# A causal mask added on VectorE instead of by a product on TensorE, in a two-layer kernel on one NeuronCore

## The reference

```
h = rms(x, ln_w)
q = (h @ wq).reshape(B, S, 32, 64); k, v = ...(B, S, 8, 64)
q, k = rope(q, k)
scores = einsum('bqhd,bkhd->bhqk', q, repeat(k, 4)) / sqrt(64)
scores = where(tril(ones(S, S)), scores, -1e30)
attn = softmax(scores, -1)
o = einsum('bhqk,bkhd->bqhd', attn, v)
x = x + o @ wo
```

## Time and profile before

| | us |
|---|---|
| median of 3 runs | 2144.54 (2142.8 to 2145.47) |
| the profiled execution | 2131.14 |
| its span, first to last instruction | 2129.3 |
| the 64-wide attention, from its first scores to its last | 828 to 1752 |

### The profile page before, as it was taken

How to read it: one execution, slowest core, us unless ns; L and a number is a source line. 1 busy time by engine, 2 the same in 40 slices (tenths; PEclk the granted TensorE clock), 3 DMA queues, 4 the chain that set the end, 5 groups by cost and what they waited for, 6 DMA issues and landing times.

```text
span 2129.3 us, 37256 instructions
## 1 busy us (share of the span) xinstructions
PE 1830.0 (86%) x11178; PEld 1224.3 (57%) x11178; DVE 1241.0 (58%) x3257; ACT 1089.9 (51%) x2758; POOL 901.9 (42%) x1013
## 2 busy tenths in 40 slices
PE   4989899867777746999999999999999994799994
PEld 2656678633333324666766666766666673555552
DVE  5684554457576755666666666666666666622222
ACT  3324343336555414666666666666666661244442
POOL 3991000112221003444554444555444552588884
PEclk9999999859999978999999999999999995899997
DMA  5000020000001010000000000000000006355557
GB/s 150 1 1 1 1 60 1 0 1 1 1 1 40 1 42 1 1 1 0 0 0 0 0 0 0 0 0 0 0 0 0 0 0 235 104 83 84 82 83 165
DMA packets 61350, 60.76 MB, mean 29 GB/s; under 512 B 13136, under 2 KB 58320, under 8 KB 61264
## 3 DMA queue, kind: packets, MB, share of 16 engines
q0 software_dynamic: 15360, 20.98, 6.2%
q1 hardware_dynamic: 45904, 38.65, 5.6%
HBM read 40.48 MB, written 19.14 MB: 28 GB/s over the span
## 4 chain that ended last, share of the span: by engine, by line
PE 53%; DVE 17%; issue 12%; ACT 11%; POOL 4%; DMA 2%; DVEq 1%; ACTq 0%; SPq 0%; POOLq 0%
PE banks L1815 5%; PE banks L1796 5%; PE banks L1805 5%; PE banks L1773 4%; PE banks L1993 3%; PE banks L1869 3%; DVE con L1024 3%; PE banks L1618 3%; ACT wide_x L1437 2%; PE banks L1844 2%; POOL wdT L724 2%; PE banks L1827 2%; ACT wugT L1451 2%; PE banks L1784 2%; PE banks L1680 2%
## 5 line engine op out<-in xcount | busy, mean ns | idle before, releaser
L1773 PE MATMUL banks<-wide_k,wide_q 128*128 128x512 f32 (+3 forms) x1024 | 314.4, 389 | 0.5 <-ACT wide_k L1390 0.5
L1024 DVE TENSOR_REDUCE con<-banks 128x1 f32<-128x256 f32 (+3 forms) x512 | 246.3, 482 | 93.4 <-PE banks L1775 90.1
L656 POOL TENSOR_TENSOR wugT<-wugT,con 128x512 f32<-128x512 f32 (+1 forms) x256 | 236.5, 934 | 141.2 <-DVE con L1014 141.1
L1815 PE MATMUL banks<-late,xnT 128*128 (+1 forms) x512 | 195.9, 506 | 17.4 <-DVE xn L1038 14.2
L1773 PEld LDWEIGHTS banks<-wide_k,wide_q 128*128 128x128 f32 x1024 | 169.9, 191 | 55.3 <-issue 24.2
L1403 ACT ACTIVATE wugT<-banks,con 128x512 f32<-128x512 f32 (+1 forms) x256 | 161.7, 632 | 67.5 <-DVE con L1024 66.3
L1054 DVE TENSOR_REDUCE con<-banks 128x2 f32<-128x1024 f32 x128 | 154.7, 1214 | 65.1 <-PE banks L1857 64.2
L667 POOL TENSOR_TENSOR attn<-attn 128x320 f32<-128x320 f32 x128 | 111.7, 872 | 169.2 <-DVE attn L1002 165.8
L1796 PE MATMUL banks<-attn 128*64 128x256 f32 x1280 | 166.4, 389 | 0.0
L1044 DVE TENSOR_TENSOR wide_x<-attn,wide_x 128x256 fp32r<-128x256 f32 (+1 forms) x256 | 97.5, 421 | 110.1 <-ACT wide_x L1437 110.1
L1993 PE MATMUL banks<-w,late 128*128 x320 | 158.1, 617 | 2.5 <-issue 1.5
(11 more groups left out here) (309 smaller groups left out, 4168.6 us busy)
## 6 DMA issues: line engine op xcount, KB each, us to landing
w<-in_L_ffn_w_dram SPq DMA_DIRECT2D x32, 256.0 KB, 6.4
late<-in_L_ffn_w_dram SPq DMA_DIRECT2D x16, 256.0 KB, 6.3
y_rows<-wqkv1T SPq DMA_DIRECT2D x1, 2176.0 KB, 7.9
x<-in_L_attn_x_dram SPq DMA_DIRECT2D x4, 512.0 KB, 8.9
late<-in_L_ffn_wq_dram SPq DMA_DIRECT2D x2, 1024.0 KB, 7.2
late<-in_L_ffn_wo_dram SPq DMA_DIRECT2D x1, 2048.0 KB, 8.2
h_rows<-wugT SPq DMA_DIRECT2D x1, 2048.0 KB, 7.0
y_rows<-x SPq DMA_DIRECT2D x1, 2048.0 KB, 12.7
```

The lines of the kernel that those rows point to most:

```text
L656: nc.gpsimd.tensor_tensor(p, p, rinv[:, m:m + 1].to_broadcast([P, n]), ALU.mult).then_inc(at.sem["norm"], 1)
L1024: nc.vector.tensor_reduce(negmax[:, a:a + 1], bank[at.sbank(a)][:, 0:P * at.keys(at.row_of(a))], AX, ALU.max, negate=True).then_inc(at.sem ...
L1773: nc.tensor.matmul(sbank[:, 0:keys], wide_q[:, side, i, qcols], wide_k[:, side, w, 0:keys], start=(w == 0), stop=False)
L1815: ins = nc.tensor.matmul(bank[YBANK][:, 0:QKV], xnT[:, c, P * wide_tile(a):P * wide_tile(a) + P], w_qkv(n, c), start=(c == 0), stop=(c == ...
```

## The change

The mask product of TensorE goes. The second score product of a unit raises s_ps instead. A bf16 tile of 512 columns, `wide_mask`, takes the place of `causal`: zero in its first 384 columns, the causal tile in its last 128. In place of the maximum, DVE runs `tensor_tensor_reduce`: it adds the last columns of `wide_mask` (as many as the unit has keys) to the scores, multiplies by -1, writes the negated masked scores back over the scores in PSUM, and accumulates their minimum, with 3e38 as the starting value, into the unit's column of `negmax`, which is the negated maximum as before. Ahead of it stands a memset of an otherwise unused column of `negmax`. The exponential takes scale -1.0, as its input is negated now.

```diff
-        causal = sb("causal", [P, P], BF16)
+        wide_mask = sb("wide_mask", [P, S], BF16)
...
-            vch.inc(nc.vector.tensor_copy(causal[:], const("causal")))
+            nc.vector.memset(wide_mask[:, 0:S - P], 0.0)
+            vch.inc(nc.vector.tensor_copy(wide_mask[:, S - P:S], const("causal")))
...
                         v.wait_ge(at.sem["s_ps"], n * at.units + a + 1)
-                        nc.vector.tensor_reduce(negmax[:, a:a + 1],
-                                                bank[at.sbank(a)][:, 0:P * at.keys(at.row_of(a))],
-                                                AX, ALU.max, negate=True).then_inc(at.sem["max"], 1)
+                        nc.vector.memset(negmax[:, 16 + a:17 + a], 0.0)
+                        kk = P * at.keys(at.row_of(a))
+                        sc = bank[at.sbank(a)][:, 0:kk]
+                        nc.vector.tensor_tensor_reduce(sc, sc, wide_mask[:, S - kk:S], -1.0, 3.0e38, ALU.add, ALU.min,
+                                                       negmax[:, a:a + 1]).then_inc(at.sem["max"], 1)
...
                     nc.scalar.activation(at.prob(m)[:, 0:n], bank[at.sbank(m)][:, 0:n], ACT.Exp, bias=negmax[:, m:m + 1],
-                                         accum_out=rowsum[:, m:m + 1]).then_inc(at.sem["exp"], 1)
+                                         scale=-1.0, accum_out=rowsum[:, m:m + 1]).then_inc(at.sem["exp"], 1)
...
                         for w in range(2):
-                            nc.tensor.matmul(sbank[:, 0:keys], wide_q[:, side, i, qcols], wide_k[:, side, w, 0:keys],
-                                             start=(w == 0), stop=False)
-                        ins = nc.tensor.matmul(sbank[:, keys - P:keys], ident_h[:], causal[:], start=False, stop=True)
+                            ins = nc.tensor.matmul(sbank[:, 0:keys], wide_q[:, side, i, qcols], wide_k[:, side, w, 0:keys],
+                                                   start=(w == 0), stop=(w == 1))
                         ins.then_inc(at.sem["s_ps"], 1)
```

## The result

The changed kernel takes 2183.8 us (median of 4 runs, 2176.71 to 2185.14) against 2143.75: ratio 1.0195, 95% interval 1.0172 to 1.0218. It is slower by 40 us. The forecast was 2152, slower by 8, with a range up to 2178.

A forecast was written before the change was run, and what follows sets the result against it. A path of DVE and ACT was taken to bound 40% of the round, so +0.48 us there less 0.26 kept on TensorE gave +0.22 us a round, +7.2 us in all: 2152 us, range 2118 to 2178.

The forecast's parts named there:

- Together DVE gets 16 x 0.14 = 2.2 us more a round: On DVE: memset and accumulator's read at 0.07 us each, 16 times a round, bringing DVE to 21.9 of 29.2 us.
- B: Rival: DVE's small instructions cost as much as ACT's record shows, 0.4 us a maximum; +46 us, 2190 us; chance 0.09.
- TensorE's slot: On TensorE: each removed mask product frees 0.09 us, bounds 0.05 and 0.14; 16 a round, 512 in all.
- Where the gain is kept: On TensorE: only units 3, 4 and 15 keep their slot, 0.26 us a round; the other units win nothing.
- ACT and DVE path: Last wait chain of a round: 11.7 of 29.2 us on ACT and DVE alone, where PE work decides nothing.
- The main part of the new instruction: On DVE: add and running minimum written to PSUM take the maximum's time, 0 more; bounds -0.02 and +0.54 us for 512.
- The read and the memset: On DVE: 0.07 us a slot each; bounds 0 to 0.20 for the read, 0.03 to 0.15 for the memset.
- On the path: Three DVE maxima on the ACT and DVE path cost 0.16 us more each, 0.48 us a round.
- DVE per round: Sign in the profile after: DVE busy 21.5 to 22.5 us a round.
- The sum: Whole round: +0.48 - 0.26 = +0.22 us; over 31 rounds +6.8 us, with the setup +7.2.
- The prediction's own sign of being wrong: Profile after: forecast wrong if the round is shorter than 29.0 us, or the new instruction has another rate.
- Rival A: PE sets the pace and DVE's additions vanish in idle time: -0.71 us a round, -22 us, 2122 us; chance 0.34.

The follow-up runs named there:

- e8: Kernel before, with two one-column DVE memsets behind each maximum, so its DVE loop has 274 instructions like the changed kernel's: 2186.03 us, ratio 1.0208.
- e3: Changed kernel with DVE's loop body holding one round in place of two (146 instructions, 30 iterations): 2129.64 us, ratio 0.9955.
- e4: Changed kernel with DVE's loop written out, no branch back: 2122.55 us, ratio 0.9936.
- e9: Changed kernel with 64 one-column DVE memsets early in the first block, shifting its loop in the instruction stream: 2122.28 us in one execution.
- e6: Kernel before with DVE's loop written out and the mask products removed, nothing in their place (scores not masked): 2116.86 us, ratio 0.9878.
- e5: Kernel before with DVE's loop written out, otherwise unchanged: 2134.91 us, ratio 0.9965.
- e7: Kernel before with DVE's loop written out, all of the change on DVE and ACT, mask product kept: 2136.97 us, ratio 0.9981.
- e12: Changed kernel with the 64 early one-column DVE memsets once more, the same kernel as e9, now timed: 2124.06 us, ratio 0.9924.

## Why the prediction was wrong

**The step that failed** is the one that ends in "Together DVE gets 16 x 0.14 = 2.2 us more a round" (the memset and the accumulator's read): the added instructions were priced by their slots on the engine and not by their count in the loop's body. 64 more instructions in two rounds brought the body from 210 to 274, and that costs some 54 us in this place of the stream (the stall is shown by e8, e3, e4 and e9; 1.6 us of each goes to TensorE's clock). The prediction put this term at nothing without a word on it, and none of the rivals had it. B came near in time, 2190, by a mechanism that isn't there.

**TensorE's slot**: taken as 0.09 us, and right. Between the first and the second qkv product e6 gains 0.27 us, and three mask products stood there, those of units 3, 4 and 5: 0.09 each, of which 0.07 to 0.08 lie at the slot itself.

**Where the gain is kept**: right for units 6 and 7, whose stretch with its hand-over takes 4.02 us in every kernel, and right in the main for the ACT and DVE path, which gives 0.07 us for its products. Wrong for unit 5. The prediction said that L1815 at 1217.44 waits for L1038; but L1038 ended at 1217.09, 0.35 us earlier, and L1815 follows the products with v directly (0.58 us in e5 and e6 alike). So unit 5 was won like units 3 and 4. The part to the first qkv product gives 0.07 as well, where nothing was counted, and the last stretch 0.05. The sum was 0.26 us forecast and 0.47 measured: the places were too few, and the slot was not too small.

**The main part of the new instruction at 0**: right, 8 and 13 ns. **The read and the memset** at 0.07 us a slot each: too much; the three instructions of a maximum take 0.01 to 0.02 us more in a dense stretch. **On the path** 3 x 0.16 = 0.48 us were forecast, and e7 has 0.15 there (11.75 to 11.90), 0.05 each if all three pay. The stretch was right and the size three times too large. PE waits for L1047 1.1 us a round (forecast 1.0), and so it is in the kernel with no stall; the waits view of e9, 1000 to 1600 us (there it is L1050):

```profile
PE banks L1832 <- DVE wide_x L1050: 23.7, 42, 0.7
```

The same wait is 0.5 us a round in e5, 0.8 in e7 and 1.0 in e6, which has no work added on DVE: most of its growth is PE arriving sooner.

**DVE per round**: 21.5 to 22.5 us were forecast; the undisturbed round shows 20.0.

**The sum** of +0.22 us a round was thus of the wrong sign for the work itself, which is -0.27 against an equal base and -0.4 to -0.5 in loops. The prediction's own sign of being wrong, a round shorter than 29.0 us, is there in every round without a stall. Rival A, PE's pace, named that side and gave 2122, near the times of e4 and e9. That is luck in part: A wanted 0.71 us less a round with the path's products won in full and DVE's additions at nothing, and the runs show 0.27 to 0.48 less, 0.07 for the whole path, and +0.20 from DVE; e4 also has the 0.2 us that writing the loop out gives. The direction of the forecast came out right by a cost that it didn't have, and that is luck too.

## What to carry to other kernels

Count the instructions of a loop body on each engine before and after an edit, and not only their durations. Here 32 short instructions more in a round made every branch back wait 3.4 us for its instructions, and cost the clock behind it. The page shows it in the row of the instruction queue and the chain as a long "issue" right behind a branch; a shorter body, a body written out, or another place of the same body takes it away. In comparing two kernels with such loops, first bring both into a form in which no branch waits for a fetch, or the place decides and not the edit.

## What the runs showed that I had not expected

- A loop of 274 DVE instructions stalls 3.4 us at its branch at two places of four, 64 instructions apart and alternating. That fits a period of one packet, 128 instructions; what exactly decides is open, since shifts in finer steps weren't tried.
- Instructions written out for 30 rounds (some 2,900 on DVE) show no stall, and save 0.2 us a round that the branch and its register arithmetic took (3.70 to 3.50 us in the first stretch, e5).
- TensorE idle for 2.8 us comes back at a granted clock of 0.60 over the next 4.3 us; it adds 1.6 us to what the wait itself costs.
- On DVE an add and a multiplication by -1 with a running minimum, from PSUM and SBUF to PSUM, take 695 ns for 512 columns where a plain maximum takes 687. The accumulator's read, 140 ns by its record, and the memset take 0.01 to 0.02 us of the engine's time together in a dense stretch.
- The changed kernel with 64 memsets more (e12) is faster than both: 2124.06 us, ratio 0.9924, against 1.0195 without them. Where its loop lies in the instruction stream is worth 2.7%.
